# A two-layer graph network on one core: SyncE fetches 29 chunks of source rows instead of 4, and the gathers lose their waits on TensorE's dense products

## What is computed

```python
# layer 0: relational graph convolution, 32 edge types, 4 bases
coeff = w_comp[etype]                                 # (E, 4)
msg_b = einsum('ei,bio->ebo', x[src], weight)
msg   = einsum('ebo,eb->eo', msg_b, coeff) * edge_weight[:, None]
x     = layernorm(x + relu(segment_sum(msg, dst) + bias))
# layer 1: normalised convolution with self loops
deg   = segment_sum(ew, dst)                          # ew: weights, and 1 for the loops
h     = x @ W
x     = layernorm(x + segment_sum((ew / deg[dst])[:, None] * h[src], dst) + b)
```

## Time and profile before

| | us |
|---|---|
| median of 3 runs | 2797.74 (2797.61 to 2799.75) |
| span of the profiled execution (first to last instruction) | 2042.2 |
| lies around it (median less span) | 755.5 |

### The profile page before, as it was taken

How to read it: one execution, slowest core, us unless ns; L and a number is a source line. 1 busy time by engine, 2 the same in 40 slices (tenths; PEclk the granted TensorE clock), 3 DMA queues, 4 the chain that set the end, 5 groups by cost and what they waited for, 6 DMA issues and landing times.

```text
span 2042.2 us, 61156 instructions
## 1 busy us (share of the span) xinstructions
PE 1497.4 (73%) x21470; PEld 1196.1 (59%) x21470; DVE 1288.6 (63%) x3623; ACT 856.8 (42%) x2171; POOL 1495.6 (73%) x1590
## 2 busy tenths in 40 slices
PE   3785566655765776777677687778778788888986
PEld 2554444544554655566566566566667667677854
DVE  8886555756557555666655575565765656477647
ACT  5563343534444443444344344443444434344313
POOL 7777777777777777777777777777777777777750
PEclk7898777878787888888888898899999999899998
DMA  5544434434334455445444545554355554455695
GB/s 135 156 148 149 141 103 142 140 128 134 92 128 140 121 152 156 147 128 152 142 121 136 147 107 160 148 151 142 105 155 157 165 163 110 122 179 141 198 346 187
DMA packets 197569, 299.93 MB, mean 147 GB/s; under 512 B 66502, under 2 KB 137083, under 8 KB 191135
## 3 DMA queue, kind: packets, MB, share of 16 engines
q1 hardware_dynamic: 99496, 167.96, 23.3%
q0 software_dynamic: 50112, 51.41, 12.9%
q10 hardware_dynamic: 47671, 76.76, 12.4%
HBM read 187.43 MB, written 108.56 MB: 145 GB/s over the span
## 4 chain that ended last, share of the span: by engine, by line
PE 33%; POOL 29%; issue 19%; DMA 9%; DVE 3%; ACTq 3%; ACT 2%; DVEq 1%; POOLq 1%
POOL gathered_rows L824 29%; DMA gathered_rows<-in_x,idx 8%; PE coefs_ps L1383 4%; PE types_ps L1259 4%; PE coefs_ps L1349 3%; PE node_ps L1259 3%; PE sums_ps L1259 3%; PE sums_ps L1283 3%; PE dense_ps L1259 3%; PE sums_ps L1296 3%; ACTq L648 2%; ACT room L1056 1%; PE node_ps L1269 1%; PE sums_ps L1360 1%; PE coefs_ps L1244 1%
## 5 line engine op out<-in xcount | busy, mean ns | idle before, releaser
L824 POOL DMA_INDIRECT gathered_rows<-in_x,idx x1559 | 1475.7, 947 | 477.5 <-issue 426.7
L1283 PE MATMUL sums_ps<-gathered_rows,chunk_factors 128*32 128x64 f32 x3118 | 98.3, 253 | 407.0 <-DMA gathered_rows<-in_x,idx 218.7
L1897 DVE TENSOR_TENSOR first_room<-first_room,dve_ps 128x1024 bf16<-128x1024 bf16 x585 | 365.0, 679 | 0.0
L1283 PEld LDWEIGHTS sums_ps<-gathered_rows,chunk_factors 128*32 128x32 f32 x3118 | 63.1, 125 | 423.2 <-issue 208.6
L1056 ACT COPY room<-dense_ps 128x294 f32 x390 | 168.8, 433 | 332.1 <-PE dense_ps L1259 277.5
L985 ACT COPY parts<-sums_ps 128x128 f32<-128x128 f32 x196 | 52.0, 265 | 465.6 <-PE sums_ps L1283 462.3
L1919 DVE TENSOR_TENSOR dve_ps<-coefs_ps,edges 128x32 f32<-128x32 f32 x196 | 38.6, 197 | 330.7 <-PE coefs_ps L1244 326.2
L1259 PE MATMUL dense_ps<-first_room 128*128 128x245 bf16 x1170 | 219.2, 301 | 31.8 <-DVE first_room L1897 31.6
L1056 ACT COPY room<-node_ps 128x294 f32 x390 | 168.8, 433 | 168.1 <-PE node_ps L1259 61.8
L1891 DVE TENSOR_TENSOR first_room<-dve_ps,first_room 128x1960 bf16<-128x1960 f16 (+2 forms) x260 | 238.7, 939 | 0.0
L1259 PE MATMUL sums_ps<-first_room 128*128 128x245 bf16 (+1 forms) x1170 | 233.8, 312 | 0.0
(11 more groups left out here) (300 smaller groups left out, 2470.4 us busy)
## 6 DMA issues: line engine op xcount, KB each, us to landing
acc_room<-block_table ACTq DMA_DIRECT2D x147, 374.5 KB
block_table<-room SPq DMA_DIRECT2D x11, 2621.5 KB
type_rows<-in_edge_type SPq DMA_DIRECT2D x260, 96.0 KB
gathered_rows<-in_x,idx POOLq DMA_INDIRECT x1559
block_table<-room SPq DMA_DIRECT2D x9, 2247.0 KB
block_table<-room SPq DMA_DIRECT2D x9, 1872.5 KB
block_table<-room SPq DMA_DIRECT2D x10, 1498.0 KB
acc_room<-block_table ACTq DMA_DIRECT2D x43, 321.0 KB
```

The costliest lines, as they stand in the source:

```text
L824: pool.indirect_dma_start(gathered_rows[:, s, j, 0:D], None, rows, bass.IndirectOffsetOnAxis(ap=idx[:, s, j:j + 1], axis=0)).then_inc(rows ...
L1283: last = nc.tensor.matmul(parts_ps[lane:lane + LANE, D * k:D * k + D], chunk_factors[:, q, c, :], rows, start=True, stop=True)
L1897: last = nc.vector.tensor_tensor(lo_hot[:, w, q0:q1, :, :], lo_hot[:, 2, q0:q1, :, :], part_of_weights(w), ALU.mult)
```

## The change

SyncE now fetches a chunk in every second iteration: `FETCHES` is 2, and the chunks are those of iterations 3, 5, ... 59, 29 in all. The even iteration before fetches 72 rows, the chunk's own iteration 56. There are two buffers, and the first row of a chunk waits for the reading of the chunk before the last. The waits of the gathers for dense products are gone.

```diff
-FETCHES = 4
+FETCHES = 2
 MIXED_UNTIL = FIRST_REGULAR
-FETCH_UNTIL = TURNED_AT[1] + 2
+FETCH_UNTIL = TURNED_AT[-1] - 1
 FETCHED = [i for i in range(FETCHES, FETCH_UNTIL) if i % FETCHES == FETCHES - 1]
-FETCHED_ROWS = (24, 40, 32, 32)
+FETCHED_ROWS = (72, 56)
...
-GATHERED_BEHIND = {2: 5, 4: 8, 6: 9}
...
-        fetched_rows = sb("fetched_rows", [P, D])
+        fetched_rows = sb("fetched_rows", [P, 2, D])
...
-                if v == 0 and n:
-                    sp.wait_ge(rows_read, FETCHED[n - 1] * U + U + FREE)
+                if v == 0 and n > 1:
+                    sp.wait_ge(rows_read, FETCHED[n - 2] * U + U + FREE)
...
-                        sp.dma_start(fetched_rows[p:p + 1, :].bitcast(u8), x_bytes[:, bass.ds(at, D * 4)]).then_inc(rows_fetched[n % 2], 16)
+                        sp.dma_start(fetched_rows[p:p + 1, n % 2, :].bitcast(u8), x_bytes[:, bass.ds(at, D * 4)]).then_inc(rows_fetched[n % 2], 16)
...
                 for j in range(chunks):
-                    if behind_dense and j in GATHERED_BEHIND:
-                        pool.wait_ge(dense_summed, step * CH + (FREE_HOTS - CH + GATHERED_BEHIND[j]))
-                        pool.sem_inc(gathers_paced, 1)
                     pool.indirect_dma_start(gathered_rows[:, s, j, 0:D], None, rows,
...
-                    rows = fetched_rows[:, :] if fetched is not None and c == chunks - 1 else gathered_rows[:, s, c, 0:D]
+                    rows = fetched_rows[:, fetched % 2, :] if fetched is not None and c == chunks - 1 else gathered_rows[:, s, c, 0:D]
```

More of the change, by code:

```diff
@@ L204 @@
 assert sum(FETCHED_ROWS) == P and len(FETCHED) <= 32 and FETCHED[-1] < ITERS - 1
-assert 2 * FETCHES > FIRST_REGULAR + 1 and max(GATHERED_BEHIND.values()) <= 2 * CH
 assert 0 < TAIL <= CH and FIRST_TILE[-1] == TILES and GROUPS <= 2 * P
@@ L472, in gnn_two_layers @@
         gathers_begun = sem("gathers_begun")
-        gathers_paced = sem("gathers_paced")
         counts_reset = sem("counts_reset")
@@ L813, in _, with gather_group @@
                            allow_small_or_imprecise_dtypes=True).then_inc(consts_ready, 1)
-            def gather_group(step, s, chunks, rows, behind_dense=False):
+            def gather_group(step, s, chunks, rows):
                 pool.wait_ge(idx_ready, step + 1)
@@ L834, in _, with gather_iter @@
             with pool.If(early == 1):
-                def gather_iter(m, v, chunks, behind_dense=False):
+                def gather_iter(m, v, chunks):
                     for s in range(U):
-                        gather_group(m * (FETCHES * U) + (v * U + s), s, chunks[s], x[:, :], behind_dense)
+                        gather_group(m * (FETCHES * U) + (v * U + s), s, chunks[s], x[:, :])
                 whole, but_one = (CH, CH, CH), (CH, CH, CH - 1)
@@ L847, in _ @@
                     for v in range(FETCHES):
-                        gather_iter(m, v, but_one if v == FETCHES - 1 else whole, True)
+                        gather_iter(m, v, but_one if v == FETCHES - 1 else whole)
                 with pool.Fori(FETCHED[-1] + 1, ITERS) as i:
                     for s in range(U):
-                        gather_group(i * U + s, s, CH, x[:, :], True)
+                        gather_group(i * U + s, s, CH, x[:, :])
                 gather_group(ITERS * U, 0, TAIL, x[:, :])
```

## The result

| | us |
|---|---|
| kernel before, median of 4 runs | 2798.74 (2797.61 to 2801.72) |
| changed kernel, median of 4 runs | 3280.27 (3271.06 to 3284.51) |
| ratio | 1.172, 95% interval 1.170 to 1.174 |
| profiled execution of the changed kernel: total, span | 3271.06, 3269.3 |

The forecast was 2804 us, 2777 to 2838. The change costs 482 us where 6.5 were expected.

What follows compares the result with a forecast made beforehand. GpSimd was taken as full for 1950 us, TensorE as setting the pace late. The 31.2 us gain counted nothing; SyncE's lateness, 15 - 8.5 = +6.5, made 2042.2 into 2048.7; with 755.5 outside the span, 2804 us (2777 to 2838).

Steps and rivals of the forecast that it cites:

- The six waits removed per iteration: GpSimd's gathers: removing their waits on TensorE was put at zero, since gaps were 0.30 us with or without a wait.
- That cover stays: GpSimd's gathers: if TensorE were far behind, the lists of indices would be late too and still hold GpSimd.
- The 755.5 us between span and the median: Whole run: the difference between the profiled span and the 2797.74 us median, left unchanged and added to the new span.
- The part that gains: GpSimd: 25 gathers leave it, 29 chunks fetched instead of 4, at 1.249 us each: 31.2 us.
- SyncE: 0.334 us a row, 58.4 us a pair: SyncE's single-row transfers: 0.334 us a row (bounds 0.326 and 0.343), so two iterations take 58.4 us, filling its waiting time.
- Where the lateness lands: TensorE's reading of fetched chunks: late at iterations 57 (12.6 us) and 59 (7.2 us); +6.5 us at the last group.
- The block store: SyncE's queue: the store now waits behind 72 rows, with 7 us left to land; its lateness was put at nothing.
- The rule of the Trainium skill: Choice of issuing engine: SyncE's path generally faster, winning 31.2 us; indirect patterns to GpSimd, making the move wrong.
- Rival 2: SyncE's queue from iteration 20: ScalarE's second queue slows rows, 0.343 or 0.35 us each; 2833 us or somewhat more; chance 0.30.
- Rivals 1 and 3: 1: TensorE rides over lateness, GpSimd stays the bound, about 2781 us, chance 0.25. 3: TensorE sets the end, 2797 us.
- The bounds: Range 2783 to 2838 us: row time moves 26 pairs by -26 (half let through) or +31, batch closings -11 or +18.
- Signs: Expected after: SyncE's type waits near zero, pairs 58 to 59.5 us, fetched-row waits every second iteration, GpSimd's list waits tens of us.

Runs made afterwards that it cites:

- the run with spaced gathers: The changed kernel with a 128x64 fill behind each gather from iteration 8 on, GpSimd waiting for each fill's end: 3129.29 us, 1.133 of before.
- quick execution: The kernel before, unchanged, in the fast kind of execution shown on the page ahead of the prediction: span 2042.2 us.
- the paced variant: The changed kernel with the gathers' waits for dense products put back from iteration 8 on: 2956.81 us, 1.057 of before.
- the run with own waits: The kernel before without the gathers' waits for dense products, plus a 128x64 fill behind each gather that GpSimd waits for: 3162.36 us, 1.145 of before.

## Why the prediction was wrong, point by point

- **"The six waits removed per iteration (with their counters) cost nothing now: the gaps of rows 2 are equal. So I put them at zero."** This is the step that failed, with 301 of the 482 us (323 where the 29 chunks are fetched as well: 2956.81 to 3280.27). The reading of the earlier trace rows was right for that execution: the waits were over before GpSimd came to them. In the executions whose times are given TensorE is behind, the waits hold GpSimd for some 500 us, and without them it gathers eight in a run, beside which TensorE starts its instructions one every 0.72 us and then loses its full clock. "That cover stays" was said of the lists of indices only; that a wait can shield another engine was in no rival.
- **"The 755.5 us between span and the median I leave as they are."** A quarter of the time was set aside as lying outside the program. A second profile shows 1.8 us there (2792.93 less 2791.1). The 755.5 us were the notice that page and times belong to different kinds of execution. All sums on GpSimd as the bound rest on taking the page for the timed runs.
- **The part that gains, 31.2 us.** Not seen as such. Where GpSimd is not the bound, the 25 chunks taken off it, together with the four that were fetched by rows, are worth 55 us (3098.44 to 3043.44, pacing off in both, no single rows in the second; each of the two ratios is known to 1%, so the 55 are rough). There are fewer gathers, though no fewer stretches of stalls (133 and 138).
- **SyncE: 0.334 us a row, 58.4 us a pair.** This is the second step that failed, with 159 us at least. The working was right for a SyncE that isn't stalled: 4 inner loads and 72 rows 28.3 us, 3 loads and 56 rows 21.8 by my numbers, 28.53 and 21.96 us measured in the run with spaced gathers. In the changed kernel it was 45.86 and 31.13. Both bounds (0.326 and 0.343) came from four stretches of one quick execution; the spread between kinds of execution was not in them. The pair came to 93.4 us there and 96 in the mean.
- **Where the lateness lands.** Not a few late chunks from iteration 57 on, but the first ones: TensorE waits for the 14 chunks up to iteration 29, 151 us, and hardly for any later one; in the paced variant for 22, 235 us. The 1.5 us put down for a row's landing was near: the sums begin 1.0 to 1.2 us after the last issue.
- **The block store, "I take nothing".** This was right: ScalarE's clearing of the room, the copy that needs the store to be through, sat idle 3.5 us in all in the changed kernel, in 2 of 65 times, and 3.6 us more stand behind a store at the copies of chunks. ScalarE's large wait (1255.0 us) is at those copies, which wait for TensorE's products.
- **The rule of the Trainium skill that was weighed** ("DMA: Bandwidth & Descriptors", section Issuing engine by pattern): the half that gives indirect patterns to GpSimd holds here, 159 us against moving 25 chunks by rows to SyncE. "Perfetto Trace Analysis", section DMA Optimizations, says that balancing DMAs across the engines that can issue them may help where descriptor generation is the bottleneck; on these executions it wasn't, and the trace that seemed to show so was of the other kind.
- **Rivals.** Rival 2 had a right place and direction for the smaller half (SyncE slower by more) and a wrong mechanism and price: no second queue, since the rows are as slow ahead of iteration 8 (0.55 to 0.60 us with their loads), but stalls; 0.57 us a row, not 0.35. Rivals 1 and 3 fall.
- **The bounds.** A half of -26 with -11 us, and +31 with +18, make 2780 to 2853 around 2804, not 2783 to 2838. The measured time lies far outside both.
- **Signs.** SyncE's waits for types near zero: 96.2 us in all, right. A pair of 58 to 59.5 us: wrong. Waits for fetched rows every second iteration: right up to iteration 29, wrong for iteration 58. GpSimd's wait for lists "tens of us, most after 1650": 1306 us, some 110 to 140 in every 300 us.

**Open.** What makes a chip stall or not; what it is in a gather that holds the other engines' instructions, its own time on GpSimd or its 32 packets; what the changed kernel would take on a quick one, and whether the removed waits cost nothing there; whether distance or GpSimd's own wait ends the stalls; why the paced gathers of the kernel before do less harm than a wait ahead of each. No version beat the kernel before.

## What to carry to other kernels

Hold the span of a profile against the median of the times before anything else: a gap of a quarter is not "around" the program, it means that the profile shows another execution than the one you are to predict, and every slack read from it is in doubt. A wait that costs nothing in one profile may be there for the runs in which it isn't free; removing it is priced by what the engine does once released, and by whom that disturbs. Where several engines show idle time "<-issue" at one common step, look for what a third engine does at that time, and test it by thinning that engine's work out, even at a price in time. Leave a first part of the run as it was: it tells in the same execution that the disturbance was there to be removed. And where a mean duration grows, part it by the granted clock before anything else is made of it.

## What the runs showed of the hardware

- On four of five chips, beside gather instructions on GpSimd, one every 1.14 to 1.33 us, TensorE and SyncE start their instructions in steps of 0.70 to 0.74 us (or twice that), from some 4 us into a run. It doesn't depend on rows (16 or 128) or bytes (64 or 256 a row). With 1.92 us between gathers, and GpSimd waiting for itself in each gap, there is none of it, while the same executions have it ahead of the first such gap. Which of the two ends it, distance or wait, is not shown.
- The same kernel takes 2763.57, 2762.38, 2769.99 or 2797.34 us on four chips, where stalls show, and 2050.66 on a fifth, where the two traces that were taken have none.
- The longer matmuls are the clock's. One matmul of the group above takes 256 to 262 ns in the mean at full granted clock and 365 to 385 at half of it, with stalls or without. The means of 258, 312 and 327 ns are mixtures: 99% of the group at full clock in the quick execution, 58% in the kernel before, 47% in it without pacing. The clock's mean over the whole span does not tell this: it is 0.746 in the run with own waits, whose group (259 ns) is at full clock for 97%, and 0.780 in the kernel before.
- A wait of GpSimd for its own fill holds the next gather 0.5 us longer than the usual gap of 0.30 us (0.81); a fill and a drain behind each gather put the gathers 3.3 us apart instead of 1.25.
